# Look-ups and index writes two groups ahead of the bias sums in the first gather stage of a GNN kernel

## The reference, cut to what matters

```python
edge_index = jnp.stack([src, dst])
x = _layernorm(x + _L0_gnn_ref(x, src, dst, ...))          # two attention layers, the first 4 heads x 16
x = _layernorm(x + _L1_gnn_ref(x, edge_index, W, b))       # mean over incoming edges
x = _layernorm(x + _L2_gnn_ref(x, edge_index, edge_attr, ...))
x = _layernorm(x + _L3_gnn_ref(x, edge_index, W, att, bias))
# inside L0, for each attention layer:
e = leaky_relu(el[src] + er[dst], 0.2)
alpha = softmax of e over the edges with the same dst
rst = segment_sum(feat[src] * alpha, dst) + bias
```

## Time and profile before

| | us |
|---|---|
| median of 3 runs | 2471.84 |
| lowest and highest | 2467.99, 2473.29 |
| the profiled execution | 2472.98 |
| its span in the trace | 2471.2 |

### The profile page before, as it was taken

How to read it: one execution, slowest core, us unless ns; L and a number is a source line. 1 busy time by engine, 2 the same in 40 slices (tenths; PEclk the granted TensorE clock), 3 DMA queues, 4 the chain that set the end, 5 groups by cost and what they waited for, 6 DMA issues and landing times.

```text
span 2471.2 us, 32119 instructions
## 1 busy us (share of the span) xinstructions
PE 1932.7 (78%) x7888; PEld 1297.1 (52%) x7888; DVE 1718.3 (70%) x6541; ACT 1118.5 (45%) x3061; POOL 1380.7 (56%) x1388
## 2 busy tenths in 40 slices
PE   3999998974777778847755665999995899959883
PEld 2888988873664223336645654566563222235552
DVE  6444444448775887669968896799895566678773
ACT  0322222223665556625535554566664555524332
POOL 4777777740002667700037773377666777727776
PEclk9655556665556777755558786999998555556555
DMA  4555555535224567624449775343531999923441
GB/s 149 168 154 154 155 157 158 156 130 199 107 107 145 168 174 208 189 79 149 150 132 245 214 214 160 93 130 129 168 119 62 315 367 316 308 80 104 127 138 29
DMA packets 268830, 401.92 MB, mean 163 GB/s; under 512 B 94344, under 2 KB 110881, under 8 KB 268517
## 3 DMA queue, kind: packets, MB, share of 16 engines
q1 hardware_dynamic: 217684, 311.07, 38.6%
q0 software_dynamic: 43904, 75.95, 11.6%
q10 hardware_dynamic: 7056, 12.85, 1.4%
HBM read 222.04 MB, written 185.39 MB: 165 GB/s over the span
## 4 chain that ended last, share of the span: by engine, by line
POOL 16%; DVE 13%; issue 11%; ACT 8%; PE 3%; DMA 2%; POOLq 0%; SPq 0%; DVEq 0%; ACTq 0%
POOL ring L659 8%; POOL out_dram L665 4%; POOL big L659 4%; ACT outr L721 4%; DVE stats L675 4%; DVE G L1149 3%; ACT big L1794 2%; DVE mv L684 1%; DVE z L1521 1%; DVE z L1864 1%; DMA ring<-x_t,idx 1%; ACT big L1802 1%; ACT hT L1780 1%; DVE z L1673 1%; PE bank L1537 0%
## 5 line engine op out<-in xcount | busy, mean ns | idle before, releaser
L659 POOL DMA_INDIRECT ring<-in_x_dram,idx x392 | 379.3, 968 | 147.4 <-issue 118.9
L721 ACT ACTIVATE outr<-z,rn 128x128 f32<-128x128 f32 x784 | 322.6, 483 | 301.2 <-DMA out_dram<-outr,idx 111.5
L659 POOL DMA_INDIRECT ring<-x_t,idx x280 | 268.5, 959 | 304.6 <-SPq L303 210.3
L659 POOL DMA_INDIRECT ring<-hidden_e,idx x196 | 193.6, 988 | 313.8 <-DVE idx L1403 256.8
L665 POOL DMA_INDIRECT x_t<-outr,idx x196 | 234.3, 1195 | 160.7 <-ACT outr L721 114.9
L1149 DVE TENSOR_TENSOR_SCAN G<-cont,G,bank 64x512 f32<-64x512 uint8 (+1 forms) x192 | 240.6, 1253 | 37.6 <-PE bank L1227 32.4
L665 POOL DMA_INDIRECT out_dram<-outr,idx x196 | 194.3, 991 | 103.1 <-issue 58.5
L1925 PE MATMUL bank<-DB,z 20*128 20x512 f32 x196 | 201.3, 1128 | 22.8 <-DVE outr L1379 7.0
L1021 DVE BATCH_NORM_STATS2 stats<-ring 128x6 f32<-128x128 f32 x196 | 42.8, 281 | 247.2 <-DMA ring<-in_x_dram,idx 247.1
L1227 PE MATMUL bank<-ident,msg 128*64 128x128 f32 (+1 forms) x588 | 151.9, 412 | 73.9 <-DVE msg L1134 71.0
L1537 PEld LDWEIGHTS bank<-W_s,G 65*128 65x128 f32 (+1 forms) x784 | 163.9, 308 | 64.7 <-issue 62.2
(11 more groups left out here) (383 smaller groups left out, 4577.1 us busy)
## 6 DMA issues: line engine op xcount, KB each, us to landing
hT<-in_x_dram SPq DMA_DIRECT2D x194, 256.0 KB
x_t<-outr SPq DMA_DIRECT2D x98, 256.0 KB, 2.9
ring<-x_e SPq DMA_DIRECT2D x98, 256.0 KB, 4.3
x_t<-xload SPq DMA_DIRECT2D x48, 512.0 KB, 3.5
xsrc_e<-ring SPq DMA_DIRECT2D x49, 256.0 KB, 2.6
xd_e<-ring ACTq DMA_DIRECT2D x49, 256.0 KB, 2.7
ring<-xsrc_e SPq DMA_DIRECT2D x49, 256.0 KB, 3.5
x_t<-xT SPq DMA_DIRECT2D x49, 256.0 KB, 4.0
```

The costliest lines, as they stand in the source:

```text
L659: nc.gpsimd.indirect_dma_start(to(c), None, table, bass.IndirectOffsetOnAxis(ap=idx[:, kind, (g + 1) * GT + c:(g + 1) * GT + c + 1].bitcas ...
L721: ins = nc.scalar.activation(to[:, k, :], frm[:, k, :], ACT.Identity, bias=sc[:, k, 1:2], scale=sc[:, k, 0:1])
```

## The change

Nothing is computed otherwise, and the number of instructions of each kind is the same. In stage c:

- VectorE: `hot`, `pick` and `hid` run ahead. Before the loop stand `hot(0)`, `hot(1)`, `pick(0)`, `hid(0)`, `hot(2)`, `pick(1)`, `hid(1)`. A turn g is then `hot(g+3)`, `pick(g+2)`, `hid(g+2)`, `shifted(g)`, where it was `hot(g+1)`, `pick(g)`, `shifted(g)`, `hid(g)`.
- Node rate steps: at the end of turns 8, 17, 26, 35 and the scaling at 36, for 9, 11, 13, 15 and 16.
- ScalarE: `copy(g-3)` in turn g, for `copy(g-1)`; the square roots at the end of turns 8, 17, 26, 35, for the start of turns 9, 11, 13, 15.
- SyncE: `codes` one group further ahead, four before the loop and between them the first two `load`.
- TensorE and GpSimd: as before.

```diff
-            extra = {9: node[0], 11: node[1], 13: node[2], 15: node[3], 16: scaled}
-            hot(0)
+            extra = {8: node[0], 17: node[1], 26: node[2], 35: node[3], 36: scaled}
+            for n in range(LEAD):
+                hot(n)
+                if n:
+                    pick(n - 1)
+                    hid(n - 1)
             for g in range(NG):
-                if g + 1 < NG:
-                    hot(g + 1)
-                pick(g)
+                if g + LEAD < NG:
+                    hot(g + LEAD)
+                if g + LEAD - 1 < NG:
+                    pick(g + LEAD - 1)
+                    hid(g + LEAD - 1)
                 shifted(g)
-                hid(g)
                 if g in extra:
                     extra[g]()
...
-            extra = {9: nroot[0], 11: nroot[1], 13: nroot[2], 15: nroot[3]}
+            extra = {8: nroot[0], 17: nroot[1], 26: nroot[2], 35: nroot[3]}
...
-            for g in range(NG + 1):
-                if g in extra:
-                    extra[g]()
+            for g in range(NG + 3):
                 if g < NG:
                     factors(g)
-                if g:
+                if 0 < g <= NG:
                     local(g - 1)
                 if g < NG:
                     apply(g)
-                if g:
-                    copy(g - 1)
+                if g >= 3:
+                    copy(g - 3)
+                if g in extra:
+                    extra[g]()
...
-            for g in range(3):
+            for g in range(4):
                 codes(g)
-            for g in range(2):
-                load(g)
+                if g < 2:
+                    load(g)
             for g in range(NG + 2):
-                if g + 3 < NG:
-                    codes(g + 3)
+                if g + 4 < NG:
+                    codes(g + 4)
```

More of the change, by code:

```diff
@@ L1382, in c_vector @@
             ch = Chain(v)
+            LEAD = 3
             def hot(n):
```

## The result

The changed kernel takes **2727.2 us** (median of 4 runs, 2724.8 to 2731.2), the kernel before 2472.6 us beside it: a ratio of 1.103, 95% interval 1.102 to 1.105. It is slower by 255 us. The profiled execution has a span of 2726.5 us, 255.3 us more than before.

What follows compares the result with a forecast made beforehand. Stage c was taken as paced by GpSimd's gathers, with 28 us lost. The new order's serial rounds gave 788.4 + 473.8 + 11 + 15 = 1288.2 us against 1058.0, +230 on 2473: 2703 us, range 2625 to 2740.

Steps and rivals of the forecast that it cites:

- The loop: Stage c: each `shifted` leads to the next through ScalarE, TensorE and VectorE, one 10.3 us round per group, formerly three groups.
- the smaller signs: Stage c's profile after: GpSimd idle about half of the stretch, gathers in fours with holes of about 5 us.
- The parts of the round: Stage c, `shifted` to `shifted`: 2.97 us to TensorE's `factors`, TensorE 2.67 to 4.93, VectorE 2.60 or 2.88.
- The clock: TensorE in stage c: idle time gives a low or falling clock, 10.3 us a round, between 9.83 and 10.78.
- the node steps: VectorE, turns 8, 17, 26, 35: 4.9 us over for the first, 2 us each later, 11 us in all.
- the sum: Stage c's end: 788.4 + 473.8 + 11 + 15 = 1288.2 us against 1058.0, so +230 us.
- the tail: Stage c after `shifted(46)`: freeing copy, last gather issues, landing and last copy, 15 us.
- The two rows on which I leaned: TensorE's trace before: granted clock 0.52 after idle times of 2.18 us and 3.92 us.
- The faster rival: Stage c: gathers stay the pace, issued without a hole, 245 us for 272.9, kernel 2445 us; chance 0.04.
- 28 us were lost: Stage c before: gathers took 272.9 us where 196 at 1.25 us need 245; nearly all laid to node steps.

## Why the prediction was right

The forecast was 2703 us, 2625 to 2740; measured 2727. The steps in its order:

- **The loop.** Right. TensorE's `factors` wait for ScalarE's in 47 of 49 groups, 4.04 us in a usual one (3 to 4 forecast); `apply` waits for the bias sum in 47; the first pick waits for TensorE 6.98 us (5 to 7 forecast). Taking TensorE's look-ups ahead, or undoing VectorE's order, removes all of it; one group less of look-ahead does too. Two of the smaller signs were off: GpSimd is idle 65% of the stretch, not about half, and its holes are 6.2 us, not 5.
- **The parts of the round.** From the bias sum to TensorE's `factors` 2.99 us (2.97 forecast), TensorE 4.95 (4.93 at the low clock), VectorE 2.97 (2.88): 10.91 us against 10.78 for the low clock.
- **The clock.** This is the term that was mis-sized. I took 10.3 us, half-way between a falling and a low clock; the clock was low in the whole part that counts, and the round was the low one. From TensorE's `factors` to the end of its look-ups, in the round shown above:

```profile
1003.30:1010.20 6.90, 6.87 (x13) 2.10 (x13) 1.88 (x6) 0.96 (x4) 3.78 (x4) 0.50 0.41 118
```

The stage became 255 us longer where 230 was forecast. The rounds without the node steps came to 27 us more than the 473.8 us of the sum, the node steps to 3 us less, the tail to 1 us more: of the 27, 22 are the clock (10.78 us for 10.3), and the rest is that the parts are 0.13 us longer than their rows. The two rows on which I leaned had idle times of 2.18 and 3.92 us; the round's 4.04 us is beside the second, behind which the clock was low from the start, so the half-way value had no row of its own. The cited passage of the Trainium skill (TensorE: Matmul & The Clock Gate, "HAM oscillation — how this bites in real kernels"), by which short bursts of matmuls with a wait in each turn are slowed in every turn, gave the better number here: 10.78 us a round and 2725 us. The run with extra matmuls agrees: the same work with the idle time filled ran at 0.97.

- **The sum.** `shifted(0)` at 788.01 us (788.4 forecast), `shifted(46)` at 1296.62. The 46 rounds with the node steps took 508.6 us, 484.8 forecast. The node steps were 4.15, 2.19, 1.36 and 0.5 us over a round, 8.2 in all (11 forecast, 4.9 of it for the first). The first three rounds hold no copy and took 10.50 us each. The tail from `shifted(46)` to the end of the last copy was 16.3 us (15 forecast).
- **The faster rival.** Its mechanism exists, and was mis-sized: with the loop open the gathers do set the pace, but at 257 us, not 245, and the kernel takes 2455 us, not 2445. I used 1.25 us from one issue to the next throughout; the mean is 1.31, since 26 of the 196 issues take over 1.0 us (up to 1.55 us, and one 2.81).
- **What the undone order shows beside this.** I held that 28 us were lost, nearly all to the node steps. The trace of the kernel before has four holes in its gathers, one for each step: 7.61, 5.45, 4.94 and 2.86 us, 21 us in all. The other 7 were mostly longer issues, 23 of the 196 over 1.0 us, which I had not read. With the order undone the holes are gone and the longer issues cost 12 us: the stretch is 16 us shorter, the kernel 14.

## What to carry to other kernels

A look-ahead on one engine alone is paid for by the others: if the consumer reads group g+2 ahead of a piece of group g, and the producer makes g+2 behind something that waits for that piece, two pipelines that each overlap become one serial round per group. Here each group that VectorE's picks ran ahead took one group out of the round: three, two, one, and three again once TensorE ran ahead as well. Write down the circle of waits and count how many groups one round carries; the time for a group is the round over that count. It cost nothing here while it was below the pace of the busiest queue (two groups, 4.07 us against 5.0), and all above it counted (one group, 10.91 us). The clock came on top: the idle time that the loop makes kept the granted clock low, which made the round itself 10.91 us, where it was 8.36 with the idle time filled. When all engines are less busy than before, follow the brackets round until they come back to where they began, and don't take the longest wait for the cause: here 292 us of GpSimd waiting for copies could be taken away for a gain of at most 8 us.

## What the runs showed of the hardware that was not expected

- Adding work made the round shorter: 24 matmuls of 384 columns, 4.08 us, in a gap of 4.04 us took the granted clock from 0.55 to 0.97, TensorE's other part from 4.95 to 2.73 us and the round from 10.91 to 8.36 us.
- The issue of an indirect gather is not of fixed length, and the load of the transfers does not explain it. Its mean was 950 ns in the changed kernel and 999 with the copies one behind, with the transfers busy 0.35 and 0.32 of the time; it was 988 in the kernel before (0.65) and 1006 with the order undone (0.67). What differs is what VectorE does beside it. With the copies one behind, all 40 issues that overlap both a bias sum and a `hot` took 1.15 to 1.43 us, as the first here, and all 134 that overlap only picks or nothing of VectorE's took 0.94 or 0.95 us:

```profile
999.36 0.69 DVE L1411 TENSOR_TENSOR z<-ring,biasc 128x512 f32<-128x512 f32 x1
999.72 1.16 POOL L659 DMA_INDIRECT ring<-hidden_e,idx  x1 [6.01 <-DVE idx L1404]
999.97 0.35 DVE L1388 TENSOR_SCALAR hT<-hT,pcol 128x512 bf16<-128x512 bf16 x1
...
1001.18 0.94 POOL L659 DMA_INDIRECT ring<-hidden_e,idx  x1 [0.30 <-issue]
```

No issue beside picks alone or beside nothing took over 1.0 us in the traces of the kernel before and of the undone order either. No run takes one of these pieces away, so which of them holds the issue up is not shown.

- Chips differed by 18% on the same kernel before: 2470 us on one, 2919 and 2916 us on two others, with 156 against 110 GB/s in the first stage. The pieces of stage c's round took the same time: TensorE's part at the low clock is 4.95 us in the changed kernel and 4.95 us (1112.08 to 1117.03) with the copy moved, on a slow chip. Why those chips move less is not known.
